# Attention that masks on the vector engine, with key 0 and query 0 inside the bands, and q and k stored by step

## The reference, cut to what matters

```
x = x + attention(layernorm(x)):                  # 16 heads of 16, S = 512
    Q, K, V = split_heads(h @ W + b)
    scores = Q K^T / 4 + mask                     # 0 where |i-j| <= 64, or i == 0, or j == 0; else -inf
    out = softmax(scores) V @ Wo + bo
x = x + ffn(layernorm(x)):                        # 16 experts, 512 tokens each, picked by top-k over tokens
    h = gelu(xg @ Wg^T) * (xg @ Wu^T);  eo = (h @ Wd^T) * weight, added at the tokens' rows
    plus a shared gated mlp on all tokens
```

## Time and profile before

| | |
|---|---|
| median of 3 runs | 1398.01 us (1396.7 to 1398.82) |
| the profiled execution, its own time | 1400.23 us |
| its span, first to last instruction | 1398.5 us |
| TensorE, weight loads, VectorE, ScalarE, GpSimd busy | 90%, 76%, 61%, 43%, 42% of the span |
| mean granted clock of TensorE | 0.952 of full speed |

### The profile page before, as it was taken

One profiled execution on the slowest core, in us unless ns is written; L12 is line 12 of the kernel. 1 busy time (PEld: TensorE's weight loads), 2 busy tenths in 40 slices (PEclk: granted clock), 3 DMA queues, 4 the chain that ended last, 5 costly groups with the idle time before them and its releaser, 6 DMA issues. The chain is left out here.

```text
span 1398.5 us, 26404 instructions
## 1 busy us (share of the span) xinstructions
PE 1256.7 (90%) x9930; PEld 1066.7 (76%) x9930; DVE 849.4 (61%) x1510; ACT 597.1 (43%) x1023; POOL 584.9 (42%) x530
## 2 busy tenths in 40 slices
PE   2995999999999972699999599999999999999997
PEld 2884777777777752588887578888888888888886
DVE  7874555555555512695688676666666666666641
ACT  1340544444444442354222255455455454545442
POOL 6000333332333342462200146666666666665554
PEclk9996999999999985699999789999999999999999
DMA  2778555555555416441003144434444433344411
GB/s 84 262 249 136 79 88 90 86 86 92 93 93 93 71 50 198 144 149 57 15 31 121 51 161 121 115 105 113 120 121 121 121 111 105 109 114 121 121 31 15
DMA packets 71284, 148.44 MB, mean 106 GB/s; under 512 B 14736, under 2 KB 31520, under 8 KB 64928
## 3 DMA queue, kind: packets, MB, share of 16 engines
q1 hardware_dynamic: 58544, 128.39, 35.4%
q0 software_dynamic: 12656, 18.90, 7.4%
HBM read 104.53 MB, written 42.21 MB: 105 GB/s over the span
## 5 line engine op out<-in xcount | busy, mean ns | idle before, releaser
L610 ACT ACTIVATE pt<-ps_p 128x512 f32<-128x512 f32 (+1 forms) x320 | 170.0, 582 | 218.1 <-PE ps_x L673 122.7
L550 DVE TENSOR_REDUCE mx<-ps_s 128x2 f32<-128x384 f32 (+2 forms) x160 | 143.9, 900 | 171.9 <-PE ps_x L651 154.9
L1803 POOL TENSOR_TENSOR h_lo<-h,h_hi 128x512 fp32r<-128x512 f32 x128 | 175.5, 1383 | 136.1 <-ACT h_hi L1839 135.8
L454 POOL TENSOR_SCALAR_AFFINE_SELECT pt<-pt 128x512 f32<-128x512 f32 x192 | 110.1, 597 | 273.4 <-ACT pt L610 273.4
L1913 PE MATMUL ps_gu<-xt_hi,w_hi 128*128 128x512 f32 x512 | 203.5, 397 | 2.1 <-DVE xt_lo L1862 2.1
L1913 PE MATMUL ps_gu<-xt_lo,w_hi 128*128 128x512 f32 x512 | 200.8, 392 | 0.0
L1913 PE MATMUL ps_gu<-xt_hi,w_lo 128*128 128x512 f32 x512 | 200.3, 391 | 0.0
L1878 DVE TENSOR_TENSOR h<-ge,ps_gu 128x512 f32<-128x512 f32 x128 | 87.8, 686 | 180.1 <-ACT ge L1833 167.9
L1740 DVE TENSOR_TENSOR w_lo<-w,w_hi 128x768 fp32r<-128x768 f32 x128 | 173.5, 1360 | 31.3 <-ACT w_hi L1735 27.8
L648 PE MATMUL ps_s<-ks,qs 96*128 96x256 f32 (+2 forms) x512 | 171.6, 398 | 0.0
L1812 POOL DMA_INDIRECT out<-ys,idx x64 | 131.1, 2049 | 73.3 <-ACT ys L1849 61.8
(11 more groups left out here) (221 smaller groups left out, 2891.9 us busy)
## 6 DMA issues: line engine op xcount, KB each, us to landing
w<-in_We SPq DMA_DIRECT2D x48, 1024.0 KB, 4.9
qk_parts<-qk SPq DMA_DIRECT2D x8, 2048.0 KB, 7.7
qs<-qk_parts SPq DMA_DIRECT2D x96, 128.0 KB, 3.6
ks<-qk_parts SPq DMA_DIRECT2D x96, 128.0 KB, 5.0
x<-in_x SPq DMA_DIRECT2D x16, 512.0 KB, 8.7
attn_t<-on SPq DMA_DIRECT2D x32, 256.0 KB, 3.7
ot<-attn_t SPq DMA_DIRECT2D x32, 128.0 KB
rd<-rden SPq DMA_DIRECT2D x16, 256.0 KB
```

Of the source, the lines that this page charges most:

```text
L454: last = pool.affine_select(out=part, in_=part, pattern=[[0, HQ], [sign, hi - lo]], compare_op=ALU.is_ge, fill=0.0, base=0, channel_multip ...
L550: last = dve.tensor_reduce(mxu[:, h:h + n, j], tile[:, :, 0:N0 if j == 0 else W[j]], AX, ALU.max)
L610: act.activation(pt[i][:, t % 2, h:h + nh], ps_p[:, n % 2].rearrange("p (h q) -> p h q", h=nh)[:, :, 0:W[i]], ACT.Exp, scale=SCALE).then_i ...
L1803: pool.tensor_tensor(h_lo[:, m], h32[:, (e * KI + m) % HB], h_hi[:, m].bitcast(F32), ALU.subtract).then_inc(hlo_s, 1)
```

## The change

1. **Layout.** q, k and their DRAM scratch get a row of 4 x 129 elements instead of 512: after each 128 columns stands a copy of column 0 (GpSimd writes it in the projection). A window of a band, now two columns wider, thus contains key 0 or query 0, and the products of two columns, `ps_x`, `far` and the activation for `pq` go. The weights' columns are permuted on the host so that the scratch is ordered [batch, step, part, element of head, head, column].
2. **Store of the projection.** Instead of one transfer a batch, eight (part c by half m), each with the destination `"t d h q -> t (d h) q"`, and an x load: nine a batch. They wait for GpSimd's copy.
3. **Loads of attention.** Four transfers a step instead of six, of 16 or 32 rows of 8256 bytes.
4. **Masks.** The scores lose the mask matmul; VectorE adds the mask and takes the maximum in one `tensor_tensor_reduce` per head and tile (16 a step), from a ring of three one-bank tiles. TensorE waits for it at each score matmul.
5. **Exponents** go in pairs of heads; ScalarE also copies the maxima of tile 0 to the added columns of `qs` (`far_rows`), for which TensorE waits once a step. GpSimd's select goes in pieces of 64 columns (11 a step).
6. **Loops** of attention are unrolled, and `wait_alone`'s counting goes there.
7. **Experts:** TensorE runs slices 0 to 6 of token tiles 0 and 1 before slice 7 of both.

```diff
+RING = 3
+ZC = P + 1
+ZS = NT * ZC
...
+WZ = [w + 2 for w in W]
+SIDE = ZC + 1
+FAR = [0, WIN + SIDE, WIN, WIN]
+UPPER = [0, SIDE, SIDE, ZC]
...
-        d["qk"] = scratch("qk_parts", (B, 4, D, S))
+        d["qk"] = scratch("qk_parts", (B, UB, 4, DH, HQ, ZS))
...
-                    sp.wait_ge(qlo_s, b * 4 + 4)
-                    sp.dma_start(d["qk"][b].rearrange("c (m p) q -> p c m q", p=P),
-                                 qk[:, h].bitcast(F32)).then_inc(out_s[h], 16)
+                    sp.wait_ge(z_s, b + 1)
+                    for c in range(4):
+                        for m in range(KD):
+                            dst = d["qk"][b, m * UB // KD:(m + 1) * UB // KD, c].rearrange("t d h q -> t (d h) q")
+                            sp.dma_start(dst, qk[:, h, c, m].rearrange("p k i -> p (k i)").bitcast(F32)).then_inc(out_s[h], 16)
...
+                for b in range(B):
+                    pool.wait_ge(qlo_s, b * 4 + 4)
+                    rows = qk[:, b % 2].rearrange("p c m k i -> p (c m) k i")
+                    pool.tensor_copy(rows[:, :, :, P], rows[:, :, 0, 0:1].to_broadcast([P, 4 * KD, NT])).then_inc(z_s, 1)
...
+                    for dst, row, part, n in ((qs, 0, 0, 1), (qs, DH, 0, 2), (ks, 0, 2, 2), (ks, 2 * DH, 2, 1)):
+                        sp.dma_start(dst[row:row + n * DH, t].bitcast(F32),
+                                     d["qk"][b, t, part:part + n].rearrange("c d h q -> (c d) h q")).then_inc(qk_in[t], 16)
...
+                def maxima(u):
+
+                    if u >= 2:
+                        dve.wait_ge(neg_s, 2 * (u - 1))
+                    for g, (j, h) in enumerate(SCORES):
+                        dve.wait_ge(sc_s, u * SG + g + 1)
+                        n, m = (S, mask[:, 0:S]) if j == 0 else (WZ[j], mask[:, S:S + WZ[j]])
+                        dve.tensor_tensor_reduce(junk[:, (u * SG + g) % RING, 0:n], ps_s[:, (u * SG + g) % RING, 0:n], m, 1.0, -3e38, ALU.add, ALU.max,
+                                                 mx[:, u % 2, h, j:j + 1]).then_inc(mx_s, 1)
...
+                def far_rows(u):
+
+                    t = u % UB
+                    act.wait_ge(m_in[t], (u // UB + 1) * 16 * MROWS)
+                    rows = qs[M_ROW:M_ROW + 2, t]
+                    act.activation(rows.rearrange("c h (j i) -> c h j i", j=NT)[:, :, 1:3, P],
+                                   rows[:, :, 0:1].bitcast(F32).to_broadcast([2, HQ, 2]), ACT.Copy).then_inc(far_s, 1)
...
+                    if n >= RING:
+                        pe.wait_ge(mx_s, n + 1 - RING)
+                    q = tile_of(qs[0:M_ROW, t, h], j)
+                    k = ks[0:M_ROW, t, h]
+                    k = whole(k) if j == 0 else window(k, j)
+                    out = ps_s[:, n % RING]
+                    out = out.rearrange("p (k c) -> p k c", c=P) if j == 0 else out[:, 0:WZ[j]]
+                    pe.matmul(out, q, k, start=True, stop=True).then_inc(sc_s, 1)
...
+                AV = {3: 0, 5: 1, 6: 2, 7: 3}
+                for u in range(NU):
+                    for n in range(SJ):
+                        if u + 2 < NU:
+                            score(u + 2, 2 * n)
+                            score(u + 2, 2 * n + 1)
+                        exponents(u, n)
+                        if u >= 1 and n in AV:
+                            times_v(u - 1, AV[n])
...
-                    for t in range(CT):
-                        if e > 0 or t >= 2:
-                            pe.wait_ge(ys_s, e * CT + (t - 1))
+
+                    def contract(t, ks):
                         ts = slice(t * P, (t + 1) * P)
-                        c = 0
-                        for k in range(KI):
+                        for k in ks:
                             if t == 0:
                                 pe.wait_ge(hlo_s, e * KI + (k + 1))
+                            c = 3 * k
                             for l, r in three(h_hi[:, k, ts], down(w_hi, s, k), h_lo[:, k, ts], down(w_lo, s, k)):
                                 last = pe.matmul(ps_y[:, t % 2, 0:D], l, r, start=c == 0, stop=c == 3 * KI - 1)
                                 c += 1
-                        last.then_inc(y_s, 1)
+                        return last
+
+                    if e > 0:
+                        pe.wait_ge(ys_s, e * CT)
+                    contract(0, range(KI - 1))
+                    contract(1, range(KI - 1))
+                    contract(0, range(KI - 1, KI)).then_inc(y_s, 1)
+                    contract(1, range(KI - 1, KI)).then_inc(y_s, 1)
+                    for t in range(2, CT):
+                        pe.wait_ge(ys_s, e * CT + (t - 1))
+                        contract(t, range(KI)).then_inc(y_s, 1)
```

More of the change, by code:

```diff
@@ L501, in load_den @@
                 def load_den(b):
[L503 removed]
+                    for s in range(2):
+                        sp.wait_ge(out_s[s], 16 * (UB // 2) * (b + 1))
                     src = d["ot"][b].rearrange("t (h r) (c i) -> t h r c i", r=32, i=DC)[:, :, DH]
@@ L572, in reciprocals @@
                     dve.reciprocal(den[:], den[:]).then_inc(rden_s, 1)
-                for t in range(UB):
-                    maxima(0, t, t < 2)
-                maxima(1, 0, False)
-                with dve.Fori(1, B - 1) as b:
-                    for t in range(UB):
-                        maxima(*after(b, t, 1), False)
-                        if t == 3:
-                            reciprocals(b - 1)
-                for t in range(1, UB):
-                    maxima(B - 1, t, False)
+                for u in range(NU):
+                    maxima(u)
+                    if u >= 9 and u % UB == 1:
+                        reciprocals((u - 9) // UB)
                 reciprocals(B - 2)
@@ new lines, in score, with exponents @@
+                    if n >= RING:
[6 more added lines that the diff above has]
+                    pe.matmul(out, q, k, start=True, stop=True).then_inc(sc_s, 1)
+                def exponents(u, n):
+                    b, t = u // UB, u % UB
+                    i, p = TJOBS[n]
+                    if n == 0:
+                        pe.wait_ge(far_s, u + 1)
+                    if u * SJ + n >= 2:
+                        pe.wait_ge(exp_s, u * SJ + n - 1)
+                    if i == 0:
+                        for r in range(2):
+                            pe.matmul(ps_p[:, n % 2, r, 0:N0], ident16[:], mask[:, 0:N0], start=True, stop=False,
+                                      skip_group_check=True)
+                    for r in range(2):
+                        k = tile_of(ks[:, t, 2 * p + r], i)
+                        q, out = qs[:, t, 2 * p + r], ps_p[:, n % 2, r]
@@ L675, in st_job, with near @@
                     last.then_inc(st_s, 1)
-                def times_v(b, t, i, first):
+                def near(rows, v, p, i):
+                    out = ps_o[rows, LO[i]:HI[i]]
+                    if i < NT - 1:
+                        pe.matmul(out.rearrange("p (k c) -> p k c", c=WIN), v,
+                                  p.rearrange("p (k c) -> p k c", c=WIN + 1)[:, :, 0:WIN],
+                                  start=False, stop=True, skip_group_check=True)
+                    else:
+                        pe.matmul(out[:, 0:WIN], v, p[:, 0:WIN], start=False, stop=True, skip_group_check=True)
+                        pe.matmul(out[:, WIN:W[i]], v, p[:, WIN + 1:W[i] + 1], start=False, stop=True, skip_group_check=True)
@@ L693, in times_v @@
                     for h in range(HQ):
-                        rows = slice(32 * h, 32 * h + 32)
-                        v = vx[:, t % 2, i, h * VW:(h + 1) * VW]
+                        rows, v = slice(32 * h, 32 * h + 32), vx[:, s, i, h * VW:(h + 1) * VW]
                         if i == 0:
-                            last = pe.matmul(ps_o[rows, N0:S], v[0:1], pt[0][0:1, t % 2, h, N0:S], start=False, stop=True,
+                            last = pe.matmul(ps_o[rows, N0:S], v[0:1], pt[0][0:1, s, h, N0:S], start=False, stop=True,
```

350 lines of the change are left out of this document (138 added, 212 removed).

## The result

| | before | changed |
|---|---|---|
| median | 1398.41 us (4 runs, 1396.7 to 1402.39) | 1639.41 us (4 runs, 1635.0 to 1652.2) |
| profiled execution, span | 1398.5 us | 1650.5 us (its own time 1652.2) |
| TensorE, weight loads, VectorE, ScalarE, GpSimd busy | and the table above | 74%, 61%, 53%, 36%, 37% |

The ratio is 1.1734 (95% interval 1.1661 to 1.1806): 17% slower, 241 us, in place of the 1625 us forecast. The span splits by three rows that both traces have: attention's first loads (110.39 before, 404.45 after: 294.1 us later), the last copy of its result (516.1, 780.18 after, so this stretch is 30.0 us shorter), and the end (12.1 us less behind that copy). 294.1 - 30.0 - 12.1 = 252.0, the difference of the two spans.

A forecast was written before the change was run, and what follows sets the result against it. TensorE was taken to bound projection and attention, with the DMA engines next in the projection. Span 1398.5 + 289 (store) - 49 (attention) - 11 (experts) = 1627.5, so 1625 us; range 1590 to 1665.

The forecast's parts named there:

- The store: Projection: outermost dimension 2 limits each store to two engines, 44 us a batch, 289 us more.
- spreads after all: Rival, projection store: successive transfers take different engines, or the shape is handled like 128 rows; 1338 us, chance 0.11.
- three engines: Rival, projection store: three engines or partly overlapping pairs, 29 us a batch, 1505 us, chance 0.04.
- The 50 us: Projection store: rows of 2064 bytes cost a transaction more, estimated 10 to 20%, some 50 us.
- ScalarE wait for the store of the batch before the last: Projection: ScalarE waits for that store, so everything in the projection slows down to it.
- The experts: Down product: 1.1 us idle an expert filled, new wait about 0.4; net 0.7 us x 16 = 11 us less.
- Attention: Attention: mean step 9.9 us instead of 11.5, 51 us less over 32 steps, taken as 49.
- a rival at 0.04: Attention: clock falls to half as TensorE pauses at each wait; 205 us more than forecast, 1830 us, chance 0.04.
- TensorE would still work 8.2 of 9.9 us: Attention: argument against the clock falling, from TensorE's own work of about 8.2 us in a mean step of 9.9.
- The regular step: Attention: 9.4 us a step, 1.2 above the larger of TensorE's 8.2 and VectorE's 8.0.
- 3.7 us: Attention: TensorE's work a step loses 1.8, 0.5 and 1.4 us, together 3.7, going from 11.5-12 to about 8.2.
- The late maxima rows: Attention: SyncE's wait after storing reciprocals delays these rows; 2.1 us lost in each of 7 steps, 15 us.

The follow-up runs named there:

- VectorE relieved and the products spread: The combined version with VectorE's four passes of tile 0 over the first 258 columns only: 1306.26 us (one run).
- the run with the products spread: The kernel with sixteen stores, products with V behind exponents 2, 3, 5 and 7 instead of 3, 5, 6 and 7: 1347.31 us, ratio 0.9597.
- the pauses filled: The kernel with sixteen stores, with TensorE running each score matmul of tiles 0 and 1 twice: 1375.35 us, ratio 0.9797.
- the combined version: Changed kernel with one store a batch, six loads a step, products with V behind exponents 2, 3, 5, 7, no SyncE wait behind the reciprocals' store: 1310.53 us.
- the one with earlier products: The combined version with the products with V behind exponents 1, 3, 4 and 6: 1333.8 us (4 runs).
- the kernel with sixteen stores: The changed kernel with each of its eight stores a batch cut in two, outermost dimension 64 rows: 1375.02 us, ratio 0.9814.

## Why the prediction was right, and where it was off

**The store (+289 us forecast, +294 measured): right.** Two engines at 24 GB/s gave 44 us a batch and 1.4 for the x load, against 45.8. That the narrow form itself limits the engines, which I had read from shares of 0.26 and 0.18, is shown by the kernel before with only that form (42.2 us a batch with 2, 11.7 with 8). By the rule of the Trainium skill, "DMA: Bandwidth & Descriptors", section "Why a DMA increments its semaphore by 16 and not by 1", 2, 8 and 16 engines work in these kernels; the batches of 42.2, 11.7 and 9.3 us agree (the last is TensorE's pace, so it bounds the store only from above). The 12 us of stores of 64 rows, for which the rule gives 16 engines too, it doesn't explain. The rivals "spreads after all" and "three engines" are out. The 50 us that I had estimated for rows of 2064 bytes, outside the sum, were at most 29. One step was wrong without a price: I had ScalarE wait for the store of the batch before the last; the first to wait is VectorE, for the x load behind the stores in the queue (178.2 us in five batches).

**The experts (-11): right,** 11.2 us alone, by the mechanism named: 0.9 us idle an expert became 0.2.

**Attention (-49): only -30.** This is where the sum failed. The copies took 329.9 us, where 31 steps of 9.9 are 306.9. Four terms of the sum changed:

- Falls of the clock, 0 in the sum. The four pairs from 480.13 to 575.88 take 95.75 us, 16.2 more than eight steps of 9.94; with the like later it is 21.6 us. I had called this a rival at 0.04 and priced it at half clock throughout. The runs show it in part: the clock falls and comes back once in two steps, locked to them. My "TensorE would still work 8.2 of 9.9 us" did not speak against it: by the profile it is busy for 9.9 of 9.94 us in the steps before the first fall.
- The regular step: 9.94 us, where I took 9.4. VectorE was cheaper than my row made it (passes at 0.61, 0.35 and 0.28 us, 6.4 a step instead of 7.2), and its work did not set the step. TensorE's list took more than 8.2: even with VectorE relieved and the products spread it is 9.43. The term that was too small is the band matmul, 0.17 us in place of the 0.123 that I took from the experts; 24 of them make 1.2 us. Besides, I had subtracted 3.7 us from "11.5 to 12", but 11.5 was the mean with attention's four last, short steps, and the regular step of before is 12.1. The error has two sides: the last four steps gained nothing (32.8 us against 29.7). Together some 10 us.
- The late maxima rows: predicted 2.1 us once in four. With the clock out of the way it is 1.2 to 2.0 (the run with the products spread). In the changed kernel, where steps are longer and the clock moves, 7 us are left of the 15.
- The start, from the first loads to the first copy, became 4.1 us shorter (50.0 to 45.9); I had counted nothing.

291 (31 x 9.4) + 10 + 21.6 + 7 = 330. The excess of 14 us over the forecast is this: +5 for the store and +19 for attention make 24 us, less 1 at the end: 23 us between the spans, 1650.5 against the 1627.5 of the sum. The median lies 13 us below the profiled execution, which is the slowest of the four and has the lowest mean clock (0.847, the others 0.856 to 0.860); so the 21.6 us for falls hold for that one, and are likely less in the median. The last line of the sum has a slip as well: from a span of 1627.5 the median follows as 1627, since the profiled execution took 1.7 us more than its span and 2.2 more than the median, and I left out the 1.7.

The Trainium skill, "TensorE: Matmul & The Clock Gate", section "A second HAM failure mode: psum-queue depth-cycling", has TensorE pause between groups of matmuls as it cycles through PSUM banks, so that the clock swings between its two levels. The traces agree in part: the changed kernel waits for a ring of three banks and has levels 1.00 and 0.50 in turn, and no falls in the regular steps with the pauses filled. But the combined version and the one with earlier products cycle through the same ring with more waiting, and stay at 1.00 in every regular step. The price of the falls was 22 us here, not the 205 that I had worked out.

**Left open:** why transfers of 64 rows are slow (above), what of the 45.8 against 42.2 us the rows of 2064 bytes cost, what sets off the falls of the clock, and what holds up the band matmuls in a step of 9.43 us (the waits for VectorE that are left are 0.4 us a step).

## What to carry to other kernels

Read a low DMA share together with a stage that stands still as "few engines", and look at the outermost dimension of the transfer: rearranging a destination so that a dimension of 2 stands outside cost 280 us here, and one transfer of 128 rows gave it back. When TensorE is put in lockstep with another engine, look at the granted clock step by step, and try independent matmuls where the other engine is slow; try more than one place, since here one order gave 28 us and the next cost 23. And take a regular step from neighbouring steps in the middle, not from a mean that includes the ends.

## What was unexpected of the hardware

- The clock's falls lock to the program: pairs of 13.64 and 10.25 us for ten pairs in a row in the kernel with sixteen stores. Its executions ran from 1364.7 us (mean clock 0.931) to 1393.6 (0.902); with the pauses filled, 1374.0 to 1377.9. So falls of the clock also show as spread.
- A kernel in which TensorE is idle for 4.8 of 100 us kept clock 1.00, and one in which it is busy for 9.9 of 9.94 us did not.
- More work for TensorE, 1.4 us a step, made the same time.
- Stores of 64 rows kept the engines busy for 0.86 of the time at 15.7 GB/s each; stores of 128 rows run at 22.
- A pass of VectorE with a mask added and a maximum taken starts every 0.61 us for 512 columns, faster than the 0.67 us at which the read behind a plain one came before.
